# Scores two steps ahead: four PSUM banks for the scores, one for the sum over V, three work banks, and Q a stage sooner

## The reference, cut to what matters

```python
q = (x @ Wq).reshape(B, S, H, D).transpose(0, 2, 1, 3)        # 16 heads of 64
k = (c @ Wk).reshape(B, N, D, H).transpose(0, 3, 2, 1)
v = (c @ Wv).reshape(B, N, D, H).transpose(0, 3, 1, 2)
mask = jnp.all(c == 0, axis=-1)[:, None, None, :]
scores = jnp.where(mask, -jnp.inf, jnp.einsum('bhsd,bhdn->bhsn', q, k) * scale)
att = jax.nn.softmax(scores, axis=-1)
out = jnp.einsum('bhsn,bhnd->bhsd', att, v)
return out.transpose(0, 2, 1, 3).reshape(B, S, H * D) @ Wo
```

## Time and profile before

| | |
|---|---|
| median of 3 runs | 2021.64 us |
| the profiled execution, its own time | 2023.33 us |
| its span | 2021.6 us |
| busy in the span: PE, PEld, DVE, ACT, POOL | 1882.3, 1464.7, 1267.1, 1122.5, 1192.4 us |
| first attention, 13-step loop over 32 stages | about 48 to 1503 us |
| granted TensorE clock, mean of the span | 0.969 |

### The profile page before, as it was taken

The page is one execution under the profiler, slowest core; times in us unless marked ns, Lnnn a source line. Parts: engine busy times, 40 slices in busy tenths (PEclk is TensorE's granted clock), DMA queues, the critical chain, the costliest instruction groups (busy, mean ns, idle before and its releaser), DMA issues. The chain is left out here.

```text
span 2021.6 us, 42317 instructions
## 1 busy us (share of the span) xinstructions
PE 1882.3 (93%) x16013; PEld 1464.7 (72%) x16013; DVE 1267.1 (63%) x3379; ACT 1122.5 (56%) x1620; POOL 1192.4 (59%) x670
## 2 busy tenths in 40 slices
PE   6999999999999999999999999999968999679995
PEld 4777777777777777777777777777755788557774
DVE  6565667565565756675575667555535777667755
ACT  4555555555555555555555555555556899535532
POOL 4666666666666666666666666666756454124450
PEclk9999999999999999999999999999988999869996
DMA  3000000000000000000000000000000311123200
GB/s 101 2 1 18 1 5 18 1 2 4 18 1 4 4 15 2 4 18 2 4 2 18 2 5 7 2 7 2 1 21 1 116 63 52 41 54 85 71 17 25
DMA packets 56411, 41.16 MB, mean 20 GB/s; under 512 B 2517, under 2 KB 53661, under 8 KB 55197
## 3 DMA queue, kind: packets, MB, share of 16 engines
q1 hardware_dynamic: 56220, 38.57, 6.4%
HBM read 37.45 MB, written 1.11 MB: 19 GB/s over the span
## 5 line engine op out<-in xcount | busy, mean ns | idle before, releaser
L539 POOL TENSOR_TENSOR a_den<-a_den,a_probs 128x1024 f32<-128x1024 f32 x352 | 838.5, 2382 | 301.2 <-ACT a_probs L789 295.5
L789 ACT ACTIVATE a_probs<-a_scores,a_mask_col 128x1024 f32<-128x1024 f32 x416 | 463.6, 1115 | 562.7 <-PE a_scores L669 519.2
L903 DVE CUSTOM_DVE_ANT_0 a_work<-a_work,a_mask_row 128x400 f32<-128x400 f32 (+1 forms) x1024 | 564.9, 598 | 160.6 <-PE a_work L579 157.0
L685 PE MATMUL a_pv<-a_probs,a_V 128*64 128x256 f32 x3328 | 405.8, 386 | 0.0
L685 PEld LDWEIGHTS a_pv<-a_probs,a_V 128*64 128x64 f32 x3328 | 220.6, 137 | 126.5 <-issue 25.1
L669 PE MATMUL a_scores<-a_shiftT,a_pick 64*128 64x256 f32 x1664 | 236.6, 277 | 0.0
L885 DVE TENSOR_TENSOR a_Q_lo<-a_work,a_Q_hi 128x512 fp32r<-128x512 f32 x32 | 22.1, 692 | 237.5 <-ACT a_Q_hi L760 237.5
L669 PEld LDWEIGHTS a_scores<-a_shiftT,a_pick 64*128 64x128 f32 x1664 | 161.1, 186 | 0.0
L539 POOL TENSOR_TENSOR a_den<-a_probs 128x1024 f32<-128x1024 f32 x32 | 76.5, 2392 | 137.1 <-ACT a_probs L789 137.1
L903 DVE DVE_READ_ACCUMULATOR2_ANT a_maxes<- 128x1 f32 x1024 | 144.1, 141 | 0.0
L665 PE MATMUL a_scores<-a_Q_hi,m_K_hi 64*128 64x256 f32 x832 | 127.6, 299 | 12.9 <-DVE a_acc L935 9.5
(11 more groups left out here) (360 smaller groups left out, 4189.0 us busy)
## 6 DMA issues: line engine op xcount, KB each, us to landing
m_gate_rows<-gate_scratch SPq DMA_DIRECT2D x8, 1024.0 KB, 4.8
a_c_nat<-in_ctx_dram SPq DMA_DIRECT2D x8, 768.0 KB
b_c_in<-in_ctx_dram SPq DMA_DIRECT2D x8, 768.0 KB
b_c_nat<-in_ctx_dram SPq DMA_DIRECT2D x8, 768.0 KB
m_w_raw<-in_L_ffn_W_dram SPq DMA_DIRECT2D x16, 256.0 KB, 5.0
a_acc<-in_x_dram SPq DMA_DIRECT2D x8, 128.0 KB, 2.1
out_dram<-tokens SPq DMA_DIRECT2D x4, 256.0 KB, 2.3
tokens<-in_x_dram SPq DMA_DIRECT2D x1, 896.0 KB, 9.5
```

The lines of the kernel that those rows point to most:

```text
L539: nc.gpsimd.tensor_tensor(total, so_far, probs[:, buffer(c, j), :], ALU.add).then_inc(den_added, 1)
L685: last = nc.tensor.matmul(PV[HD * odd:HD * odd + HD, c % 2, queries], V[:, c % 2, j, h * HD:(h + 1) * HD], probs[:, buffer(c, j), first:fi ...
L789: nc.scalar.activation(probs[:, buffer(c, j), :].rearrange("p (o n) -> p o n", o=2), Sc[:, :, :], ACT.Exp, bias=mask_col[:, c // GROUPS % ...
L903: nc.vector.tensor_tensor_reduce(out=X[:, bank, :w], in0=X[:, bank, :w], in1=mask_row[:, off:off + w], scale=1.0, scalar=-3e38, op0=ALU.ad ...
```

## The change

Scores go into four banks, by the parity of the step, and are issued two steps ahead: slot j issues scores of step j+2, and these wait for the exponential of step j, one step earlier than before. ACT likewise does exp of step j+2 in slot j. `PV` is one bank; pv of step 0 of a stage waits for the copy of the stage before, and that copy is now at slot 0. Work banks are three. All products of the 128 x 128 form move from the wide slots to the odd ones ("groups"), behind pv, so a wide slot has scores and at most one max (stage 0: two). `q` of a stage is made two stages ahead at the end of the last group slot. The maxima have new places (`MAX_AT`): S ahead of pv, M between pv and the other products, E at the end of the slot; `MAX_FIRST` holds those of stage 0. In odd stages slot 0 has pv of the old stage, M, the products, and then pv of the new stage. The prologue's list stays as it is.

```diff
--- before.py
+++ after.py
@@ -137,17 +137,19 @@
     PIECES = [(0, 402), (402, 400), (802, 400), (1202, 400)]
     K_PIECES = PIECES[:3] + [(1202, NC * P - 1202)]
     KS, VS, MAXES = 4 * PAIRS, (NC + 1) // 2, 8 * PAIRS
-    BANKS = 4
+    BANKS = 3
     TURN = 2 * GROUPS
     FIRST_TURN, LAST_TURN = 2, 2 + 3 * TURN
 
-    COPY_STEP, SCAN_STEP = 1, 10
+    COPY_STEP, SCAN_STEP = 0, 10
     STD_STEP, SCALE_STEP = 4, 8
     EXPERT_SPLITS = [(STAGES - 4, 6), (STAGES - 3, 6)]
     K_ORDER = [0, 4, 1, 5, 2, 6, 3, 7]
-    K_AHEAD = {3: (0, 4), 4: (1, 5), 5: (2, 6)}
     K_FIRST = {0: (0, 4), 1: (1, 5, 2), 2: (6, 3, 7)}
-    V_AT = [(0, 3, 3, 1, 1, 0, 1), (0, 3, 3, 1, 0, 0), (0, 1, 1, 1, 1, 0, 1), (0, 3, 3, 1, 0, 0)]
+    V_AT = [(1, 2, 2, 2, 1, 1), (1, 1, 2, 1, 1, 1, 0), (1, 1, 2, 1, 0, 0), (1, 1, 2, 1, 1, 1, 0)]
+    MAX_AT = [{0: "S", 1: "SME", 2: "S", 3: "SME", 4: "S", 5: "SM", 6: "S", 7: "SM", 8: "S", 9: "S"},
+              {0: "SM", 1: "S", 2: "SME", 3: "S", 4: "SE", 5: "S", 6: "SM", 7: "S", 8: "SM", 9: "S"}]
+    MAX_FIRST = {2: "SS", 3: "SS", 4: "SS", 5: "SSMM", 6: "SS", 7: "SS", 8: "S", 9: "S"}
     LATE_VS = (0, 0, 2, 2)
 
     def wide(c, j):
@@ -167,53 +169,63 @@
 
         return range(VS - LATE_VS[(s - 1) % GROUPS], VS) if 0 < s < STAGES else range(0)
 
+    def previous(c, j):
+
+        return (c, j - 1) if j > 0 else (c - 1, STEPS - 1)
+
+    def k_ahead(c):
+
+        if c == 0:
+            return {3: (0, 4), 4: (1, 5), 5: (2, 6)}
+        if c % GROUPS == 2:
+            return {3: (0, 4, 1), 4: (5, 2, 6)}
+        return {2 + c % 2: (0, 4), 3 + c % 2: (1, 5), 4 + c % 2: (2, 6)}
+
     def raw_plan(c):
 
-        first, middle, last = [[[] for _ in range(STEPS)] for _ in range(3)]
-        wides = [j for j in range(STEPS) if wide(c, j)]
+        first, between, middle, last = [[[] for _ in range(STEPS)] for _ in range(4)]
         groups = [j for j in range(STEPS) if not wide(c, j)]
         s = c + 1
-        for j in groups:
-            middle[j].append((c, "pv", 0))
         vs = [(c, "v", i) for i in late_vs(c)]
         if s < STAGES:
             vs += [(s, "v", i) for i in range(VS) if i not in late_vs(s)]
-            middle[wides[0]].append((s, "q", 0))
-        ks = K_FIRST if c == 0 else {0: (3, 7)} if s < STAGES else {}
-        for w in ks:
-            middle[wides[w]] += [(s, "k", i) for i in ks[w]]
-        if s < STAGES:
-            places, taken_up = [(j, part) for j in range(STEPS) for part in (first, last)], 0
-            for m in range(MAXES):
-                made = [w for w in ks if K_ORDER[m // 2] in ks[w]] + [0]
-                taken_up = max(taken_up, 2 * wides[made[0]] + 2)
-                j, part = places[taken_up]
-                part[j].append((s, "max", m))
-                taken_up += 1
-            assert j < wides[5] - 1
-            last[wides[5] - 1].append((s, "shift", 0))
-        if has_context(c):
-            for w, i in ((1, 0), (1, 1), (2, 2), (2, 3)):
-                middle[wides[w]].append((c // GROUPS + 1, "cT" if i < 3 else "cxT", i))
-            for i in range(4):
-                middle[wides[6]].append((c // GROUPS + 1, "mask", i))
-        if has_context(c + 1):
-            last[SCAN_STEP] += [(c // GROUPS + 1, "scan", 0), (c // GROUPS + 1, "xn", 0)]
-        for w, n in enumerate(V_AT[c % GROUPS]):
-            middle[wides[w]] += vs[:n]
-            vs = vs[n:]
-        assert not vs
-        if c + 2 < STAGES:
-            for w in K_AHEAD:
-                middle[wides[w]] += [(c + 2, "k", i) for i in K_AHEAD[w]]
+        if c == 0:
+            middle[groups[0]].append((s, "q", 0))
         if c > 0:
             after_den = [j for j in groups if j >= 2][0]
             middle[after_den].append((c - 1, "den", 0))
             for i, j in enumerate((1, 3, 3, 5)):
                 last[after_den + j].append((c - 1, "recip", i))
-            middle[wides[5 if has_context(c) else -1]].append((c - 1, "proj", 0))
+            middle[groups[-1]].append((c - 1, "proj", 0))
+        if has_context(c):
+            for w, i in ((1, 0), (1, 1), (2, 2), (2, 3)):
+                middle[groups[w]].append((c // GROUPS + 1, "cT" if i < 3 else "cxT", i))
+        if has_context(c + 1):
+            last[SCAN_STEP] += [(c // GROUPS + 1, "scan", 0), (c // GROUPS + 1, "xn", 0)]
+        if s < STAGES and c % 2 == 1:
+            middle[groups[5]].append((s, "spread", 0))
+        ks = K_FIRST if c == 0 else {0: (3, 7)} if s < STAGES else {}
+        for w, n in enumerate(V_AT[c % GROUPS]):
+            late = [(s, "k", i) for i in ks.get(w, ())]
+            early = [(c + 2, "k", i) for i in k_ahead(c).get(w, ())] if c + 2 < STAGES else []
+            middle[groups[w]] += late + vs[:n] + early
+            vs = vs[n:]
+        assert not vs
         if s < STAGES:
-            middle[wides[5]].append((s, "spread", 0))
+            if c % 2 == 0:
+                middle[groups[4]].append((s, "spread", 0))
+            m = 0
+            for j, parts in (MAX_FIRST if c == 0 else MAX_AT[c % 2]).items():
+                for part in parts:
+                    {"S": first, "M": between, "E": last}[part][j].append((s, "max", m))
+                    m += 1
+            assert m == MAXES
+            first[9].append((s, "shift", 0))
+        if c + 2 < STAGES:
+            middle[groups[-1]].append((c + 2, "q", 0))
+        if has_context(c):
+            for i in range(4):
+                middle[groups[-1]].append((c // GROUPS + 1, "mask", i))
         if c == STAGES - 1:
 
             middle[0].append((s, "mw", 0))
@@ -228,7 +240,13 @@
                 middle[j].append((s, "mT", g))
             for g, j in enumerate((9, 10, 12, 12)):
                 middle[j].append((s, "ml", g))
-        return [a + b + c for a, b, c in zip(first, middle, last)]
+        slots = []
+        for j in range(STEPS):
+            products = [] if wide(c, j) else [(*previous(c, j), "pv"), (c, j, "pv")]
+            products = [(t, kind, step) for t, step, kind in products]
+            split = 1 if products and j == 0 else len(products)
+            slots.append(first[j] + products[:split] + between[j] + middle[j] + products[split:] + last[j])
+        return slots
 
     def raw_prologue():
 
@@ -252,7 +270,6 @@
         return PROLOGUE_USES + sum(PLAN_USES[:c])
 
     PER_TURN = first_use(LAST_TURN - 2 * TURN) - first_use(FIRST_TURN)
-    assert PER_TURN % BANKS == 0
 
     def numbered(slots, use):
 
@@ -325,8 +342,8 @@
         rest_squares = den[:, :, :].rearrange("p a n -> p (a n)")[:, 0:(TILES - 2) * D]\
             .rearrange("p (t d) -> p t d", d=D)
 
-        Sc = es.enter_context(nc.psum_tensor("a_scores", [P, 2, PAIRS * S], F32))
-        PV = es.enter_context(nc.psum_tensor("a_pv", [P, 2, PAIRS * S], F32))
+        Sc = es.enter_context(nc.psum_tensor("a_scores", [P, 2, 2, PAIRS * S], F32))
+        PV = es.enter_context(nc.psum_tensor("a_pv", [P, PAIRS * S], F32))
         X = es.enter_context(nc.psum_tensor("a_work", [P, BANKS, 512], F32))
 
         x_loaded, rest_loaded, c_loaded = sem("x_loaded"), sem("rest_loaded"), sem("c_loaded")
@@ -374,9 +391,6 @@
         def steps_of(it, c, first):
             return at(it, TURN * STEPS, c * STEPS + first)
 
-        def has_next(it, c):
-            return it is not None or c + 1 < STAGES
-
         def items_of(slots, s, kinds):
             return [use + n for slot in slots for t, kind, _, use in slot if t == s and kind in kinds
                     for n in range(uses(kind))]
@@ -399,9 +413,9 @@
 
             return 8 if wide(c, 1) else 9
 
-        def previous(c, j):
-
-            return (c, j - 1) if j > 0 else (c - 1, STEPS - 1)
+        def ahead(c, j):
+
+            return (c, j + 2) if j + 2 < STEPS else (c + 1, j + 2 - STEPS)
 
 
         @block.sync
@@ -652,8 +666,8 @@
 
             def scores(it, c, j):
 
-                if c > 0 or j > 0:
-                    pe.wait_ge(probs_done, steps_of(it, c, j))
+                if c > 0 or j > 1:
+                    pe.wait_ge(probs_done, steps_of(it, c, j - 1))
                 if j == 0:
                     all_taken(pe, it, made_before(c, ("q", "k", "spread")))
                 keys = slice(j * P, (j + 1) * P)
@@ -662,11 +676,11 @@
                     for n, (left, right) in enumerate(((0, 0), (0, 1), (1, 0))):
                         for odd in range(2):
                             rows = slice(HD * odd, HD * odd + HD)
-                            nc.tensor.matmul(Sc[:, odd, queries], K[c % 2][left][rows, p, keys],
+                            nc.tensor.matmul(Sc[:, (c * STEPS + j) % 2, odd, queries], K[c % 2][left][rows, p, keys],
                                              Q[c % 2][right][rows, queries], start=(n == 0), stop=False)
                     for odd in range(2):
                         rows = slice(HD * odd, HD * odd + HD)
-                        last = nc.tensor.matmul(Sc[:, odd, queries], pick[rows, p, :], shiftT[rows, c % 2, :],
```

(34 more changed lines are left out.)

## The result

The changed kernel takes 2136.47 us (median; 2132.49 to 2139.0) where the kernel before takes 2022.61 beside it (2018.86 to 2024.44): a ratio of 1.056 [1.0545, 1.0576], 114 us slower. The direction was as predicted; the time is 36 us above the forecast of 2100 and 11 above the upper end of the range.

What follows compares the result with a forecast made beforehand. PE was taken to bound the attention. Per turn -1.1 - 4.5 + 14.2 + 0.9 = +9.5 us, +71 over stages 1 to 30; with +6.3, +6.7 and -3, +81: forecast 2100 us, range 2045 to 2125.

Steps and rivals of the forecast that it cites:

- part 2: Scores two steps ahead: PE's waits for exp and at odd stages' ends vanish, inside 4.5 us a turn; no new wait.
- Part 3: Three work banks, the main term: waits for banks to return add 14.2 us a turn, bounds 4.7 and 18.
- max-scores-max: Two maxima with scores between take 1.31 us, not 1.13: 0.18 lost at each place, 4.7 a turn.
- M behind two reciprocals: M's bank returns late behind a pair of reciprocals on DVE: 0.56 us, four times, 2.3 a turn.
- E behind k3, k7, v: In even stages the E max waits for k7's bank: 0.65 us, twice, 1.3 a turn.
- k7: Products behind M: k7 waits 0.38 us for M's first bank, four times, 1.5 a turn.
- Part 4: One PV bank: in even stages pv of step 0 waits 0.47 us for ACT's copy, twice, 0.9 a turn.
- Part 1: PE's changes of array form: 10 entries at 0.20 us fewer, 6 at 0.14 more, -1.1 us a turn.
- Part 5: The ends: prologue +6.3 us with rounds of 3.85, stage 0 +6.7, stage 31 -3.
- rival 3: Scores behind a max cost 0.10 extra, 1.2 GHz clock lasts longer early (13 us): +95 to +110, up to 2130; chance 0.1.
- 1 (faster): Banks return in time; only form changes and the scores' lead count: 2013 us, or 1977; chance 0.11.
- 2 (half): Only some of the bank waits and the PV copy show: +4.8 us a turn, +46, 2068 us; chance 0.2.

Runs made afterwards that it cites:

- e1: The changed kernel with the shift written by a tensor_reduce (min over a pair) instead of a tensor_scalar: 2101.28 us, ratio 1.038.
- e3: The kernel before with three work banks instead of four, nothing else changed: 2180.42 us, ratio 1.076.
- e2: The changed kernel with DVE reducing only the first half of each work bank's columns in the maxima: 2034.29 us, ratio 1.006.
- e5: The kernel before with DVE reducing only the first half of each work bank's columns in the maxima: 2004.65 us, ratio 0.991.
- e10: The changed kernel with half of the columns reduced and the shift written by tensor_reduce: 2026.35 us, ratio 1.001.
- e7: The changed kernel with the shift written by tensor_reduce and, in even stages, ACT's PV copy ahead of exp of step 2: 2095.97 us, ratio 1.036.
- e4: The kernel before with the transposed shift ahead of the two K pieces instead of behind proj: 2012.5 us, ratio 0.995.

## Why the prediction was right in direction and short in size

**What failed: in part 2, the sentence "I take no new wait there", and the cover given to the shift by the "two pv blocks (1.88 us)" ahead of its transpose.** The prediction gave the write no duration. In slot 9 it meets POOL's addition in 31 of 32 stages and waits for its end, up to 2.4 us; then k or pv ends before it. Behind k and pv the transpose lost 4.06 us a turn. The sum names no such wait; if the unnamed 0.40 of its context stage is meant for it, 3.66 was missing, else all: x 7.5 = 27 to 30 us of the 34 by which the sum was short. Taking it away (e1) gives 30 us in stages 1 to 30, 35 in all. The row of before showed it: L916, median 173 ns and maximum 2250 ns. A maximum 13 times the median, on 8 values in each partition, wanted a reason.

**Part 3, three banks, had the mechanism right** (e3, and e2 with e5 and e10). e1 leaves 2101 us, 9.0 us a turn for +9.5. Term by term: max-scores-max 0.22 for 0.18 behind a stalled max, 0.14 behind a fresh one; M behind two reciprocals 0.41 for 0.56; E behind k3, k7, v 0.75 for 0.65; E behind the context's v 1.01 for 0.87; k7 0.11 to 0.20 ahead of its first matmul and 0.11 more ahead of its second, for 0.38. Left out were the transposes of the mask, which now follow one another at the end of the context stage's last slot and wait for a bank: one stands 0.81 behind the one before, where 0.11 to 0.16 is undisturbed. Whether a max pair could share one bank stayed untested: every run gives it two.

**Part 4** was right: 0.40 for 0.47, twice a turn, 0.30 of it the copy's own (e7). **Part 1**, changes of form, can't be read from the changed kernel: its turn without the waits, 194.3 - 14.5 = 179.8 against 181.5 - 4.5 = 177.0, is 2.8 longer and not 1.1 shorter. A max that has waited hands on its scores 0.26 and not 0.18 later (559.32 behind 559.06, 577.79 behind 577.61), which no step had: some 37 maxima wait in a turn, and 0.08 for each is 3.0 us of these 3.9, an estimate from these rows. That hides the form changes. Where fewer maxima wait, the difference has the forecast's sign: 181.4 - 6.8 = 174.6 us in e10 against 179.6 - 3.5 = 176.1 in e5, -1.5 for -1.1. All four waits were counted alike, without what is under 0.11 us, and are good to about 1 us, so this agrees with part 1 and doesn't show it.

**Part 5** holds the second step that failed: the prologue, whose rounds were all put at the full clock, was +11.3 for +6.3. Stage 0: +6.4 for +6.7. Stage 31: -1.3 for -3. The prologue's rounds at full clock are as forecast (columns: start, duration):

```profile
19.86 0.45 PE L593 MATMUL a_work<-m_K_hi,a_Q_hi 64*128 64x402 f32 x2 [0.68 <-ACT a_mask_row L769]
...
21.35 0.45 PE L593 MATMUL a_work<-m_K_hi,a_Q_hi 64*128 64x402 f32 x2 [1.03 <-DVE a_maxes L916]
...
21.79 0.45 PE L571 MATMUL a_work<-a_cT_hi,a_Wk_hi 128*128 128x400 f32 x1
...
22.65 0.51 ACT L775 ACTIVATE m_K_hi<-a_work 128x400 fp32r<-128x400 f32 x1 [2.76 <-PE a_work L573]
...
23.19 0.58 DVE L903 TENSOR_TENSOR m_K_lo<-a_work,m_K_hi 128x400 fp32r<-128x400 f32 x1
...
23.91 0.45 PE L593 MATMUL a_work<-m_K_hi,a_Q_hi 64*128 64x402 f32 x2 [0.27 <-DVE m_K_lo L903]
...
25.27 0.45 PE L593 MATMUL a_work<-m_K_hi,a_Q_hi 64*128 64x402 f32 x2 [0.91 <-DVE a_maxes L916]
...
27.82 0.70 PE L593 MATMUL a_work<-m_K_hi,a_Q_hi 64*128 64x400 f32 x2
...
32.72 0.70 PE L593 MATMUL a_work<-m_K_hi,a_Q_hi 64*128 64x400 f32 x2
```

The second max stands 1.36 behind the first in the second round (25.27), for 1.38; a round is 23.91 - 19.86 = 4.05 and 27.82 - 23.91 = 3.91, for 3.85. But then TensorE's granted clock is not full (windows of the changed kernel, has the columns):

```profile
18.00:28.00 10.00, 6.96 (x38) 4.61 (x37) 6.23 (x19) 3.56 (x8) 9.28 (x11) 0.95 0.29 82
28.00:48.00 20.00, 16.04 (x54) 11.71 (x54) 11.82 (x36) 4.52 (x9) 11.37 (x10) 0.51 0.00 1
```

From about 27 to 47.6 us the granted clock is 0.5, 1.2 GHz, where the kernel before has 1.00 from 18 to 40. The four rounds in it take 4.90 (32.72 - 27.82), 4.90, 5.16 and 5.17 us: 4.7 us more than four of 3.85, nearly all of the 5.0 that were missing. From 18 to 28 us PE was busy 6.96 of 10, where it was 8.20 before. This was in rival 3, at "13 us" and for a longer stretch. What makes it fall isn't settled: e2 has PE busy even less, in the windows of its profile, and holds the full clock until about 40 us:

```profile
18.00:28.00 10.00, 6.86 (x40) 4.54 (x38) 5.15 (x20) 4.34 (x9) 9.27 (x11) 1.00 0.27 78
28.00:34.00 6.00, 4.05 (x21) 2.69 (x21) 3.41 (x16) 1.36 (x3) 5.84 (x3) 1.00 0.02 4
34.00:40.00 6.00, 3.84 (x22) 2.61 (x21) 3.16 (x13) 2.25 (x4) 5.27 (x8) 1.00 0.00 0
```

**The rivals.** 1 (faster) falls: the waits are 14.5 us a turn, 10 more than before, and it needed fewer than 4 new ones. 2 (half) falls: M's and E's waits behind pv and v all show. 3 (more) was nearest in time, 2130, but by half for other reasons: its low clock came, its 0.10 behind a max showed, as a stalled max's 0.08, and the largest piece was none of its. With e1's write the forecast holds within 2 us, and that is in part luck: the prologue is 4.7 us over its term, and stages 1 to 30 are 4 us under theirs, with errors of both signs in them (M and k7 put too high, what waiting maxima hand on left out).

## What to carry to other kernels

Before an instruction of DVE is moved to another time, look at its minimum, median and maximum: a wide spread on a small tile can be a collision that its present place avoids, and the new place may not. A bank of PSUM taken from a rotation is paid by every producer whose consumer holds it longer than the producer works: write down that return time (here 0.82 us behind the start of a reduction) and lay the new order beside it slot by slot. And a lost wait can often be had without its price: the move of the transposed shift alone (e4) gave 10 us, while the change that contained it cost 114.
